# A graph network on one core: the adjacency build takes a destination as quarter and place, with a ring of eight

## What is computed

```python
h = jnp.maximum(_layernorm(x), 0.0)
x = x + _L0_gnn_ref(h, W_lin, W_agg, edge_index)   # segment_sum(h[src], dst), a mean by degree
...
x = x + _L1_gnn_ref(...)                           # the same sums, twice
...
x = x + _L2_gnn_ref(...)                           # segment_sum(h[dst], src)
...
x = x + _L3_gnn_ref(...)                           # attention over the same edges
```

## Time and profile before

| | us |
|---|---|
| runs before, median (lowest to highest) | 3345.48 (3345.35 to 3350.49) |
| span of the profiled execution | 3347.6 |
| TensorE busy in it | 2186.4 |
| VectorE busy in it | 2262.1 |
| GpSimd busy in it | 1645.1 |
| ScalarE busy in it | 846.9 |
| the build, between two readings of its windows | 359 to 850 |

### The profile page before, as it was taken

How to read it: one execution, slowest core, us unless ns; L and a number is a source line. 1 busy time by engine, 2 the same in 40 slices (tenths; PEclk the granted TensorE clock), 3 DMA queues, 4 the chain that set the end, 5 groups by cost and what they waited for, 6 DMA issues and landing times.

```text
span 3347.6 us, 46752 instructions
## 1 busy us (share of the span) xinstructions
PE 2186.4 (65%) x12603; PEld 1297.7 (39%) x12659; DVE 2262.1 (68%) x3125; ACT 846.9 (25%) x1397; POOL 1645.1 (49%) x1455
## 2 busy tenths in 40 slices
PE   0488877777895989995963444444567665528563
PEld 0233455454453455553443111111366621107563
DVE  8999898898558720055133454444987799979777
ACT  0099433232002020022100111111244322206442
POOL 7400133333047777777104777777876777710000
PEclk9799999999997999997986555565559999965897
DMA  2000010110443523400724433345348733530453
GB/s 71 0 0 0 25 49 39 44 44 39 148 137 84 164 60 96 94 1 1 158 59 94 117 113 112 112 116 104 93 153 268 240 110 110 107 37 0 134 175 94
DMA packets 195115, 301.52 MB, mean 90 GB/s; under 512 B 120540, under 2 KB 133818, under 8 KB 194922
## 3 DMA queue, kind: packets, MB, share of 16 engines
q1 hardware_dynamic: 138986, 175.88, 16.5%
q0 software_dynamic: 40512, 62.87, 10.3%
q10 hardware_dynamic: 15552, 61.94, 6.0%
HBM read 191.65 MB, written 88.01 MB: 84 GB/s over the span
## 4 chain that ended last, share of the span: by engine, by line
PE 35%; POOL 19%; issue 16%; DVE 16%; DMA 6%; ACT 5%; ACTq 1%; DVEq 0%; SPq 0%; POOLq 0%; PEldq 0%
POOL arena L1313 18%; PE PS L538 11%; PE PS L699 9%; PE PS L884 6%; DMA arena<-T_att,idx 5%; ACT arena L514 4%; DVE arena L559 4%; PE PS L981 3%; PE PS L476 2%; DVE arena L1204 1%; PE PS L968 1%; DVE arena L374 1%; DVE arena L490 1%; POOL W L1322 1%; DVE arena L567 1%
## 5 line engine op out<-in xcount | busy, mean ns | idle before, releaser
L1313 POOL DMA_INDIRECT arena<-T_att,idx x864 | 843.7, 976 | 316.9 <-issue 224.8
L538 PE MATMUL PS<-arena 128*128 128x400 f16 (+2 forms) x4320 | 782.5, 332 | 270.0 <-issue 109.7
L538 PEld LDWEIGHTS PS<-arena 128*128 128x128 f16 (+2 forms) x4320 | 529.9, 158 | 512.9 <-issue 349.8
L1148 DVE TENSOR_REDUCE arena<-PS 128x1024 f32 (+1 forms) x432 | 502.2, 1212 | 321.6 <-PE PS L1115 321.6
L1486 POOL DMA_INDIRECT order<-arena x400 | 504.8, 1262 | 246.5 <-issue 246.5
L559 DVE TENSOR_SCALAR arena<-arena 128x1600 f16<-128x1600 f16 x448 | 385.7, 905 | 64.4 <-PE PS L538 60.4
L1115 PE MATMUL PS<-arena,pick 128*128 128x512 bf16 x812 | 315.8, 488 | 157.0 <-DVE arena L1148 143.2
L699 PE MATMUL PS<-arena 128*128 128x512 f16 (+1 forms) x1575 | 317.6, 361 | 88.3 <-issue 75.2
L633 POOL TENSOR_TENSOR rdeg<-rdeg,arena 128x1600 f32<-128x1600 f32 x48 | 159.9, 3331 | 313.4 <-ACT arena L617 313.4
L1104 PE MATMUL PS<-ident_b,score_buf 128*32 128x128 bf16 x864 | 90.0, 268 | 307.1 <-ACT score_buf L1077 297.4
L699 PEld LDWEIGHTS PS<-arena 128*128 128x128 bf16 x1575 | 147.8, 99 | 254.1 <-issue 102.3
(11 more groups left out here) (257 smaller groups left out, 2786.0 us busy)
## 6 DMA issues: line engine op xcount, KB each, us to landing
spill<-arena SPq DMA_DIRECT2D x108, 560.0 KB, 2.8
arena<-spill ACTq DMA_DIRECT2D x108, 560.0 KB, 3.9
arena<-A SPq DMA_DIRECT2D x50, 800.0 KB, 4.5
A<-arena SPq DMA_DIRECT2D x50, 400.0 KB, 2.4
arena<-A SPq DMA_DIRECT2D x50, 400.0 KB, 3.2
arena<-T_att,idx POOLq DMA_INDIRECT x864
order<-arena POOLq DMA_INDIRECT x400
T_att<-h SPq DMA_DIRECT2D x2, 1600.0 KB, 12.3
```

The source lines that it names most:

```text
L538: return t.matmul(where, lhsT, rhs, start=False, stop=True, skip_group_check=True)
L1148: v.tensor_reduce(cmax[d][:, u:u + 2, bass.ds(i * SLOTS + half * GROUP + q // 2 * QUAD, QUAD)], PS[:, u * BANK:(u + 2) * BANK].rearrange(" ...
L1313: p.indirect_dma_start(out=ring1[:, b, j, :], out_offset=None, in_=T_att[d][:, :], in_offset=bass.IndirectOffsetOnAxis(ap=idx[:, d, k:k + ...
```

## The change

A destination `d` of 0..1599 within its band is taken as a quarter `q = d // 400` and a place `d - 400 q`. Beforehand, once for all chunks, `hi_i` is counted up from three comparisons of `dst_in`; `src_quarter` is the source plus 128 times the quarter, `dst_low` the place. For each chunk VectorE then makes a 512-wide one-hot of `src_quarter` (four blocks of 128, one for each quarter, and an edge has its one in one of them) and a 400-wide one-hot of `dst_low`. The four products of a chunk take four different blocks of weights by the same 400 columns. Both kinds of buffer now stand in rings of eight. The 128 x 1024 instruction for eight sources is gone, with its two preparations and its semaphore `src_ready`.

```diff
-        RING_D, RING_S, RING_A = 4, 2, 4
...
+        RING_D, RING_A = GROUP, 4
+        QW = BW // BQ
+        src_quarter, dst_low, hi_i = view(0, CH[1]), view(CH[1], CH[1]), view(2 * CH[1], CH[1])
+        oh_d = [view(7200 + s * QW // 2, QW // 2).bitcast(F16) for s in range(RING_D)]
+        oh_s = [view(8800 + s * BQ * P // 2, BQ * P // 2).bitcast(F16) for s in range(RING_D)]
...
         def build_dve(v):
             def chunk(i, s, first):
                 if not first:
                     v.wait_ge(chunk_done, RING_D * i + s - RING_D + 1)
-                v.tensor_scalar(oh_d[s], steps_h, dst_in[:, bass.ds(RING_D * i + s, 1)], None, ALU.is_equal) \
-                    .then_inc(dst_ready, 1)
-
-            def sources(i, s, first):
...
-                v.tensor_tensor(oh_s[s], iota_8, key_h[:, c].unsqueeze(1).to_broadcast([P, P, GROUP]), ALU.is_equal) \
-                    .then_inc(src_ready, 1)
+                c = bass.ds(RING_D * i + s, 1)
+                v.tensor_scalar(oh_s[s], steps_h[:, 0:BQ * P], src_quarter[:, c], None, ALU.is_equal)
+                v.tensor_scalar(oh_d[s], steps_h[:, 0:QW], dst_low[:, c], None, ALU.is_equal).then_inc(dst_ready, 1)
 
             v.wait_ge(sorted_ready, 1)
-            v.tensor_copy(iota_8, steps_h[:, 0:P].unsqueeze(2).to_broadcast([P, P, GROUP]))
-            dve_link(v.tensor_copy(key_h, key[:, 1, :]))
...
+            dve_link(v.tensor_scalar(hi_i, dst_in, float(QW), None, ALU.is_ge))
+            for q in range(2, BQ):
+                dve_link(v.scalar_tensor_tensor(hi_i, dst_in, float(q * QW), hi_i, ALU.is_ge, ALU.add))
+            v.scalar_tensor_tensor(src_quarter, hi_i, float(P), key[:, 1, :], ALU.mult, ALU.add)
+            dve_link(v.scalar_tensor_tensor(dst_low, hi_i, -float(QW), dst_in, ALU.mult, ALU.add))
+            for s in range(RING_D):
+                chunk(0, s, True)
+            with v.Fori(1, CH[1] // RING_D) as i:
+                for s in range(RING_D):
+                    chunk(i, s, False)
...
         def build_pe(t):
...
-            with t.Fori(0, GR[1] // RING_S) as i:
-                for s in range(RING_S):
...
-                            last = add_to(t, PS[:, bass.ds((turn[j] & (BQ * BANK)) + b * BANK, w)], oh_s[s][:, :, j],
-                                          oh_d[j % RING_D][:, b * w:(b + 1) * w])
+            with t.Fori(0, CH[1] // RING_D) as g:
+                turn = load_row(t, cell_turn[:, bass.ds(g * RING_D, RING_D)], 1, BQ * BANK * (BANDS - 1) + CELLS)
+                for j in range(RING_D):
+                    t.wait_ge(slot_free, turn[j] & 63)
+                    t.wait_ge(dst_ready, g * RING_D + j + 1)
+                    for b in range(BQ):
+                        last = add_to(t, PS[:, bass.ds((turn[j] & (BQ * BANK)) + b * BANK, QW)],
+                                      oh_s[j][:, b * P:(b + 1) * P], oh_d[j])
+                    last.then_inc(chunk_done, 1)
```

More of the change, by code:

```diff
@@ L199, in gnn_kernel @@
         dst_in = view(6656, CH[1])
-        RING_D, RING_S, RING_A = 4, 2, 4
-        oh_d = [view(7200 + s * BW // 2, BW // 2).bitcast(F16) for s in range(RING_D)]
-        oh_s = [view(10400 + s * GROUP * P // 2, GROUP * P // 2).bitcast(F16).rearrange("p (c j) -> p c j", j=GROUP)
-                for s in range(RING_S)]
+        RING_D, RING_A = GROUP, 4
[3 more added lines that the diff above has]
+        oh_s = [view(8800 + s * BQ * P // 2, BQ * P // 2).bitcast(F16) for s in range(RING_D)]
         stage = [view(11424 + s * BW // 2, BW // 2).bitcast(F16) for s in range(RING_A)]
-        iota_8 = view(14624, GROUP * P // 2).bitcast(F16).rearrange("p (c j) -> p c j", j=GROUP)
-        key_h = view(14624 + GROUP * P // 2, CHUNKS // 2).bitcast(F16)
         blk = view(20800, 8 * BLK).rearrange("p (x o c n) -> p x o c n", x=2, o=2, c=2)
@@ L282, in gnn_kernel @@
         apart_ready, apart_seen = sem("apart_ready"), sem("apart_seen")
-        src_ready, dst_ready, chunk_done = sem("src_ready"), sem("dst_ready"), sem("chunk_done")
+        dst_ready, chunk_done = sem("dst_ready"), sem("chunk_done")
         cell_out, slot_free = sem("cell_out"), sem("slot_free")
@@ L558, in chunk @@
                     v.wait_ge(chunk_done, RING_D * i + s - RING_D + 1)
-                v.tensor_scalar(oh_d[s], steps_h, dst_in[:, bass.ds(RING_D * i + s, 1)], None, ALU.is_equal) \
-                    .then_inc(dst_ready, 1)
-            def sources(i, s, first):
-                if not first:
-                    v.wait_ge(chunk_done, (RING_S * i + s - RING_S + 1) * GROUP)
-                c = bass.ds((RING_S * i + s) * GROUP, GROUP)
-                v.tensor_tensor(oh_s[s], iota_8, key_h[:, c].unsqueeze(1).to_broadcast([P, P, GROUP]), ALU.is_equal) \
-                    .then_inc(src_ready, 1)
-            v.wait_ge(sorted_ready, 1)
-            v.tensor_copy(iota_8, steps_h[:, 0:P].unsqueeze(2).to_broadcast([P, P, GROUP]))
-            dve_link(v.tensor_copy(key_h, key[:, 1, :]))
-            per = GROUP // RING_D
-            for s in range(RING_S):
[L575 to L584, removed]
+                c = bass.ds(RING_D * i + s, 1)
+                v.tensor_scalar(oh_s[s], steps_h[:, 0:BQ * P], src_quarter[:, c], None, ALU.is_equal)
+                v.tensor_scalar(oh_d[s], steps_h[:, 0:QW], dst_low[:, c], None, ALU.is_equal).then_inc(dst_ready, 1)
+            v.wait_ge(sorted_ready, 1)
+            dve_link(v.tensor_scalar(hi_i, dst_in, float(QW), None, ALU.is_ge))
[8 more added lines that the diff above has]
+                    chunk(i, s, False)
         def build_pe(t):
@@ L590, in build_pe @@
                 clear_bank(t, k)
-            with t.Fori(0, GR[1] // RING_S) as i:
[L592 to L601, removed]
-                            last = add_to(t, PS[:, bass.ds((turn[j] & (BQ * BANK)) + b * BANK, w)], oh_s[s][:, :, j],
-                                          oh_d[j % RING_D][:, b * w:(b + 1) * w])
-                        last.then_inc(chunk_done, 1)
+            with t.Fori(0, CH[1] // RING_D) as g:
[7 more added lines that the diff above has]
+                    last.then_inc(chunk_done, 1)
         def build_act(a):
```

## The result

The changed kernel takes **3300.06 us** (median of 4 runs, 3295.82 to 3305.75) against 3347.31 us for the kernel before (4 runs, 3345.35 to 3350.49): a ratio of 0.986, with a 95% interval of 0.9845 to 0.9875. That is 47 us less, where 55 less, 3290 us, was forecast, within a range of 3274 to 3312.

The account below looks back on a forecast made before the run. GpSimd's additions stop VectorE and TensorE waits on its ring of four, 66 us of a 487.9 us stage. 66 - 13 (branches) + 4 (weights) - 1 (beginning) = 56 us less, so 3290 us, range 3274 to 3312.

Parts of the forecast that it names:

- What bounds the kernel: Build stage, 487.9 us: GpSimd's additions stop VectorE, TensorE uses up the ring of four and waits.
- The undisturbed stage: Build at the pace of groups without waits, 7.80 us with a branch and 7.32 without: 422 us.
- the 66 us of disturbance: Rest of the 487.9 us build stage, which a deeper ring and a shorter VectorE can win.
- the 95.0 us put down to line 559: TensorE's idle time under VectorE's compare in the build; to be read with care, as gaps between groups bear that name too.
- VectorE's work: Compares of the build: 0.49 us a chunk for 0.62; with standstills VectorE needs 351 to 380 us, under TensorE's time.
- The ring of eight: Buffers between VectorE and TensorE: a 3.2 us standstill uses four chunks, regained in 3.9 us; the 66 us go.
- The seams: TensorE's register loads between groups of eight chunks: all 56 groups now have the branch, 13 us more.
- The weights: TensorE's weight loads in the build, columns now side by side, 99 ns for 146: 4 us taken as gain.
- The upper bound of 21 us: Most that packed weight loads could gain, 448 x 0.047, if all of each chunk's first load counted.
- Beginning and end: Preparations before the build's first compare: some 3.0 us for 1.0, less 0.7, so 1 us later; the end stays.
- The clock: TensorE's granted clock, 0.94 over the stage, should stay at the upper level, 2.4 GHz; nothing added for it.
- The sum: 66 - 13 + 4 - 1 = 56 us less: stage 431 us, profiled span 3291.6, median 3290 us.

Follow-up runs that it names:

- number 4: Kernel before, with GpSimd adding only 16 of a cell's 1600 columns (no standstills of VectorE): stage 425.7 us, runs of 3289.15 and 3289.86 us.
- number 2: Kernel before, with eight buffers for the 1600-wide one-hots in place of four, old compares kept: stage 433.1 us, runs 3295.22 us, ratio 0.9853.
- number 1: Changed kernel with rings of four in place of eight, new compares and packed weights kept: stage 470.8 us, runs 3338.02 us, ratio to before 0.9984.
- number 6: Changed kernel with four groups of eight chunks in one lap of TensorE's loop: stage 420.0 us, runs 3288.33 us, ratio to before 0.9822.
- number 3: Changed kernel with weight columns four elements apart in place of side by side: stage 434.3 us, runs of 3292.73 and 3302.21 us.
- number 5: Changed kernel with GpSimd adding only 16 of a cell's 1600 columns (no standstills of VectorE): stage 434.0 us, runs of 3302.97 and 3304.53 us.

## Why the prediction was right

- *What bounds the kernel.* Right. The undisturbed stage was put at 422 us and number 4 measures 425.7; the 66 us of disturbance are 62. Most of the 3.7 us between are seams longer than the two that the 422 was built from: three of about 1.8 us and five of about 1.2 in number 4. The reading that most of the 95.0 us put down to line 559 are seams held in each run: a row names who came last, and at a seam that is most often VectorE, however long it had been done.
- *VectorE's work.* Right: 0.26 and 0.23 us apart, as worked out from widths 128, 448 and 1600. The fixed part of 0.13 us held for the new widths, not the longer one that the Trainium skill gives (VectorE: DVE Perf Modes, the section on the TRN2 errata), by which an estimate for the pair is 0.55 us and not 0.49. Standstill 127 us ((615 - 345) x 448 and, with line 558's median of 314, (328 - 314) x 448 = 6) a little under the 131 to 160 forecast. VectorE's idle time is 62.6 us, within the 50 to 80, but that is in part luck: with 220 + 127 us of work, 87 of the 434.1 would be left. The paces leave out that a pair with a wait behind it is done 0.59 us after its start (504.34 to 504.61 + 0.32), not 0.49; with 176 waits that is 18 of the missing 24 us.
- *The ring of eight.* Right, and it is what the gain needs: number 2 has the gain with the ring and without the narrower compares, number 1 has a third of the stage's with them and without the ring.
- *The seams.* 13 us for 28 branches more. A branch is 0.4 us by the seams of number 6, so 11, or 14.1 / 42 = 0.34 by its stage, so 9.
- *The weights.* The upper bound of 21 us is out: number 3 gives back 18 of the 50 ns and the stage moves by 0.2 us. Whether the 4 us were right is open. The loads did shorten as forecast, from 146 to 96 ns. The nearest comparison is number 4, with columns eight apart and no standstills, plus 28 branches, 435 to 437 us, against 434.0 in number 5: 1 to 3 us for the packed weights and all else that differs.
- *Beginning and end.* 1.3 us later for the 1 forecast. Another 1.7 us is the permutation, which ended later in this execution.
- *The clock.* Right: 1.00 over the stage, but for some 3 us that are shown in the last section.
- *The sum.* A stage of 434.1 us for 431 forecast. The regular groups are as forecast: from 371.13 to 791.04 there are 54, 7.78 us each, and 7.72 without what the six long seams add; 56 x 7.72 - 1.3 = 431. The term that was mis-sized is the undisturbed stage, 422 us in the prediction and 425.7 in number 4: it had no long seams, and here the six add 3 us. The profiled span is 3295.5 us for 3291.6; of the 3.9, 3 are the stage. The rest of the miss of 10 us is not in the build. The forecast went from the profiled span to the runs by 2.1 us less; after the change the median of the runs is 4.6 us above the profiled span. Each later run stands on record some 1.8 us above its own span (3297.36 for 3295.5), so the profiled execution before lay some 4 us above the median of its runs, that of the changed kernel 3 us below its own, and these 6.7 us are scatter between executions.

## What to carry to other kernels

When one engine makes buffers for another and a third engine stops it now and then, compare the stop with the consumer's pace. Here a stop of 3.2 us is four chunks of 0.79 us: a ring of four lost 37 us (number 1) to 62 us (before), a ring of eight none when the producer had slack (number 5) and 7 us when it had not (number 2), though the stops went on unchanged. Sizes between were not tried.

Idle time that a profile puts down to the producer is only a wait if the producer was late. Look at a stretch, or a kernel, in which it is ahead; what remains there, here the seams, belongs to the consumer. A producer's share of the chain does not tell either: it was 10.3% with the waits and without them.

Once the ring covers the stops, work taken off the consumer's own instruction stream pays: here 42 branches fewer were 14.1 us, and 28 register loads fewer, of twice the words, 9.5 us more.

## What was not expected of the hardware

GpSimd waits as well as VectorE. In number 2, where VectorE is hardly ever idle, an addition takes 4137 ns on average, against 3331 before and 3216 in the changed kernel. The Trainium skill (SBUF — State Buffer, who interferes with whom) says that the two share a pair of ports as a lock, and that the one that begins second is the one that waits; the trace agrees both ways. In the changed kernel a compare that comes 0.13 us after an addition ends 0.15 us behind it. In number 2 an addition that comes at 560.10, 0.26 us after a compare had begun, takes 3.46 us, and one at 569.11, in a row of compares without a pause, 5.76.

The lower clock cost nothing in one place. In the changed kernel some ten of the 32 products of one group of eight fall into a stretch where the granted clock is 0.50, that is 1.2 GHz, after two seams of about 1.8 us. (The two other pairs of such seams, at 542 and 675 us, have no lower clock behind them, so the seams alone don't bring it.) TensorE's timeline, the window (columns as in the earlier trace rows), and the weight loads, of which one belongs to each product:

```profile
441.07 6.42 PE L536 MATMUL PS<-arena 128*128 128x400 f16 x32 [1.77 <-issue]
449.32 7.39 PE L536 MATMUL PS<-arena 128*128 128x400 f16 x32 [1.82 <-issue]
457.05 3.22 PE L536 MATMUL PS<-arena 128*128 128x400 f16 x16 [0.34 <-DVE arena L558]
```

```profile
450.60:453.00 2.40, 2.40 (x9) 1.09 (x8) 1.31 (x6) 0.00 (x0) 0.00 (x0) 0.50 0.00 0
```

```profile
451.63 0.15 PEld L536 LDWEIGHTS PS<-arena 128*128 128x128 f16 x1 [0.18 <-issue]
451.96 0.15 PEld L536 LDWEIGHTS PS<-arena 128*128 128x128 f16 x1 [0.18 <-issue]
...
453.63 2.68 PEld L536 LDWEIGHTS PS<-arena 128*128 128x128 f16 x16 [0.18 <-issue]
```

At 0.50 the products come 0.33 us apart (451.96 - 451.63), behind it sixteen in 2.68 us, 0.17 apart. That is quicker than the usual 6.42 / 32 = 0.20, so at the upper level it is not the data that sets 0.79 us a chunk: the sequencer got ahead while the products were slow. The group takes 7.39 us in place of 6.42, and the seam behind it shrinks from 1.32 to 0.34. From start to start it is 457.05 - 449.32 = 7.73 us, like any other group.
